# A routed feed-forward layer: gate and up computed by neuron instead of by slot

## What is computed

```python
mod = (silu(c) @ wmod).reshape(4, 6, 1, -1)          # shift, scale, gate, twice
h = layernorm(x) * (1 + ca) + sa
x = x + ga * attention(h)
h = layernorm(x) * (1 + cb) + sb
# experts: E = 8, H = 256, F = 704 neurons, top 2 of 8, weights w normalised
gate = silu(xt @ Wg[e].T)                            # (tokens, 704)
up = xt @ Wu[e].T                                    # (tokens, 704)
out = out + gate * up @ Wd[e].T * comb[:, e:e + 1]   # (tokens, 256)
x = x + gb * out
```

## Time and profile before

| | us |
|---|---|
| median of 3 runs | 262.04 (261.97 to 262.65) |
| the profiled execution, device time | 260.57 |
| its span, first to last instruction | 258.8 |
| TensorE busy | 221.5 |
| VectorE busy | 168.6 |
| ScalarE busy | 158.3 |
| GpSimd busy | 123.9 |

### The profile page before, as it was taken

One profiled execution on the slowest core, in us unless ns is written; L12 is line 12 of the kernel. 1 busy time (PEld: TensorE's weight loads), 2 busy tenths in 40 slices (PEclk: granted clock), 3 DMA queues, 4 the chain that ended last, 5 costly groups with the idle time before them and its releaser, 6 DMA issues.

```text
span 258.8 us, 5010 instructions
## 1 busy us (share of the span) xinstructions
PE 221.5 (86%) x1409; PEld 153.8 (59%) x1410; DVE 168.6 (65%) x417; ACT 158.3 (61%) x281; POOL 123.9 (48%) x172
## 2 busy tenths in 40 slices
PE   0898998989963139999999999999999999999970
PEld 0635576768852114665666666666666666666650
DVE  2347759998896996995776776769544444444430
ACT  2403999898956374888688888896444444444410
POOL 1126846778110081465666667664644454543222
PEclk9999997989965557999999999999999999999996
DMA  6998226717543046579369356233333333333111
GB/s 237 346 403 354 83 75 202 252 67 228 174 187 104 18 129 259 172 223 305 38 174 305 60 166 197 41 61 57 68 63 61 64 64 61 61 62 62 23 20 20
DMA packets 15203, 35.88 MB, mean 139 GB/s; under 512 B 1928, under 2 KB 9480, under 8 KB 15180
## 3 DMA queue, kind: packets, MB, share of 16 engines
q1 hardware_dynamic: 8424, 24.00, 27.0%
q0 software_dynamic: 5152, 9.08, 18.1%
q10 hardware_dynamic: 1604, 2.52, 2.8%
HBM read 30.47 MB, written 6.18 MB: 142 GB/s over the span
## 4 chain that ended last, share of the span: by engine, by line
PE 67%; DVE 11%; ACT 9%; DMA 5%; issue 4%; POOLq 1%; POOL 1%; ACTq 1%; DVEq 0%
PE bank L717 33%; PE bank L743 17%; PE bank L727 6%; PE bank L544 3%; ACT W L795 3%; ACT W L788 3%; PE bank L533 2%; DMA W<-in_wmod 2%; PE bank L707 2%; DMA out<-shared,dest_i 1%; PE bank L490 1%; PE bank L499 1%; DMA token_rows<-rows 1%; ACT W L801 1%; PE bank L481 1%
## 5 line engine op out<-in xcount | busy, mean ns | idle before, releaser
L717 PE MATMUL bank<-W,x 128*128 x414 | 87.9, 367 | 1.2 <-ACT x L924 1.2
L717 PEld LDWEIGHTS bank<-W,x 128*128 128x128 f16 x414 | 41.0, 99 | 41.8 <-issue 4.2
L1426 POOL DMA_INDIRECT out<-shared,dest_i x23 | 36.5, 1587 | 58.1 <-DVE shared L1289 58.1
L743 PE MATMUL bank<-W,shared 128*128 x414 | 49.7, 273 | 2.6 <-DVE shared L1304 1.7
L930 ACT ACTIVATE x<-bank,unscale 128x256 f32<-128x256 f32 (+1 forms) x69 | 31.3, 459 | 31.9 <-PE bank L717 31.9
L1279 DVE SCALAR_TENSOR_TENSOR shared<-bank,unscale,x 128x256 f32<-128x256 f32 (+1 forms) x69 | 30.7, 459 | 24.6 <-ACT x L930 24.3
L743 PEld LDWEIGHTS bank<-W,shared 128*128 128x128 f16 x414 | 39.5, 99 | 8.4 <-issue 3.0
L999 DVE SCALAR_TENSOR_TENSOR W<-staged,w_scale_bits,W 128x1408 f16<-128x1408 f32 (+1 forms) x24 | 42.4, 1766 | 1.0 <-ACT W L795 0.7
L795 ACT ACTIVATE W<-staged,w_scale_bits 128x1408 f16<-128x1408 f32 (+1 forms) x24 | 36.0, 1502 | 2.7 <-DVE w_scale_bits L980 1.6
L788 ACT ACTIVATE W<-staged 128x1408 bf16<-128x1408 f32 (+1 forms) x24 | 33.8, 1411 | 0.0
L1304 DVE TENSOR_TENSOR shared<-bank,shared 128x512 f16<-128x512 f32 (+1 forms) x46 | 23.5, 553 | 10.2 <-ACT shared L939 10.1
(11 more groups left out here) (171 smaller groups left out, 288.1 us busy)
## 6 DMA issues: line engine op xcount, KB each, us to landing
staged<-in_w SPq DMA_DIRECT2D x16, 704.0 KB, 5.2
staged<-in_w SPq DMA_DIRECT2D x8, 768.0 KB, 4.5
token_rows<-mod_rows ACTq DMA_DIRECT2D x1, 1036.0 KB
x<-in_x SPq DMA_DIRECT2D x4, 256.0 KB, 9.6
W<-in_wmod SPq DMA_DIRECT2D x2, 512.0 KB, 9.0
out<-x SPq DMA_DIRECT2D x4, 256.0 KB, 3.6
token_rows<-rows SPq DMA_DIRECT2D x4, 256.0 KB, 3.0
W<-in_w_in ACTq DMA_DIRECT2D x1, 896.0 KB, 7.4
```

The costliest lines, as they stand in the source:

```text
L717: mm = pe.matmul(bank[2 + n][:, 0:2 * w], half[:, kc * P:(kc + 1) * P], W1_pairs[:, bass.ds(e * 2 + part, 1), :, kc, n * PIECE:n * PIECE + w],
L743: mm = pe.matmul(bank[7][:, 0:D], a[:, fc * P:(fc + 1) * P], W2_16[:, bass.ds(e * 2 * W2_EXP + part * W2_EXP + fc * D, D)], start=(k == 0) ...
L1426: po.indirect_dma_start(out, bass.IndirectOffsetOnAxis(dest_i[:, j:j + 1], 0), y_sb[r], None, bounds_check=last_row, oob_is_err=True, comp ...
```

## The change

The diff does three things.

1. **Gate and up by neuron.** In `gate_up` 128 neurons of the weights are now the stationary operand and the 128 slots stream. A tile needs 11 chunks of 128 neurons (5.5 of gate, 5.5 of up; one chunk in the middle holds the last 64 of gate and 64 of up), each with 6 matmuls of 128 columns: 66 matmuls. The result has neurons on the partitions, so `turn_act` is gone. `act_hi` and `act_lo` are now made from `act` in SBUF by ScalarE and VectorE, in two sets of buffers, and `down` is 17 matmuls in another order, with waits inside it. It writes bank 5 or 7 in turn.
2. **One scale.** The largest bound over the four batches (`common_scales`) gives one scale for all rows. The three constants no longer travel with the rows; GpSimd's `unscales` and `slot_weights` read them from SBUF.
3. **Slots by VectorE.** `slot16` of the tiles 1 to 22 is copied from PSUM by VectorE after `mult_pieces`, instead of by ScalarE after SiLU.

```diff
@@ gate_up @@
-                terms = [(half, kc, part) for kc in range(DC) for half, part in ((slot_hi, 0), (slot_hi, 1), (slot_lo, 0))]
-                for n, w in enumerate(PIECES):
-                    for k, (half, kc, part) in enumerate(terms):
-                        mm = pe.matmul(bank[2 + n][:, 0:2 * w], half[:, kc * P:(kc + 1) * P],
-                                       W1_pairs[:, bass.ds(e * 2 + part, 1), :, kc, n * PIECE:n * PIECE + w],
-                                       start=(k == 0), stop=(k == len(terms) - 1))
+                for n in range(PIECES):
+                    if not (isinstance(i, int) and 4 * i + c < 1):
+                        pe.wait_ge(s["act_ok"], ACT_OPS * (4 * i + c - 1) + (ACT_OPS if n == PIECES - 1 else n + 1))
+                    for col, of in chunks[n]:
+                        terms = [(half, kc, part) for kc in range(DC) for half, part in ((slot_hi, 0), (slot_lo, 0), (slot_hi, 1))]
+                        for k, (half, kc, part) in enumerate(terms):
+                            mm = pe.matmul(bank[2 + n][:, col:col + P],
+                                           W1_16[:, bass.ds(e * 2 * W1_EXP + part * W1_EXP + kc * W1_ROW + of, P)],
+                                           half[:, kc * P:(kc + 1) * P], start=(k == 0), stop=(k == len(terms) - 1))
                     mm.then_inc(s["gu_done"], 1)
-
-            def turn_act(i, c):
...
@@ down @@
-                terms = [(a, fc, part) for a, part in ((act_hi, 0), (act_hi, 1), (act_lo, 0)) for fc in range(FC)]
+                hi, lo = act_hi[c % 2], act_lo[c % 2]
+                terms = [(hi, fc, part) for fc in range(FULL) for part in (0, 1)] + [(lo, fc, 0) for fc in range(FULL)]
+                terms += [(hi, FULL, part) for part in (0, 1)]
...
@@ ScalarE, tile_step @@
-                if not last(i, c):
-                    slots_out(i, c + 1)
...
-                sc.wait_ge(s["at_done"], 2 * (4 * i + c) + 1)
-                sc.activation(act_hi[:, 0:4 * P], bank[5][:], ACT.Copy).then_inc(s["act_hi_ok"], 1)
-                sc.wait_ge(s["at_done"], 2 * (4 * i + c) + 2)
-                sc.activation(act_hi[:, 4 * P:6 * P], bank[6][:, 0:2 * P], ACT.Copy).then_inc(s["act_hi_ok"], 1)
+                if not (isinstance(i, int) and 4 * i + c < 2):
+                    sc.wait_ge(s["down_done"], 4 * i + c - 1)
+                for cols, ready in ((slice(0, 2 * PIECE), PIECES - 1), (slice(2 * PIECE, FC * P), ACT_OPS)):
+                    sc.wait_ge(s["act_ok"], ACT_OPS * (4 * i + c) + ready)
+                    sc.activation(act_hi[c % 2][:, cols], act[:, cols], ACT.Copy).then_inc(s["act_hi_ok"], 1)
@@ VectorE @@
+            def common_scales():
+
+                ve.wait_ge(s["scale_in"], 16)
+                most, inverse = bounds[:, B:B + 1], bounds[:, B + 1:B + 2]
+                link(ve.tensor_reduce(most, bounds[:, 0:B], AX.X, ALU.max))
+                link(ve.reciprocal(inverse, most))
+                ve.tensor_scalar(common[:, G_ROW:G_ROW + 1], inverse, ROW_NORM, None, ALU.mult)
...
             def tile_step(i, c):
                 mult_pieces(i, c)
+                if not last(i, c):
+                    ve.wait_ge(s["xt_done"], 4 * i + c + 2)
+                    ve.tensor_copy(slot16, slots_p).then_inc(s["slot_ok"], 1)
...
+                lows(i, c)
                 if c == 0:
                     slot_weights()
-                else:
-                    result(i, c - 1, (c - 1) % 2)
...
+                if c:
+                    result(i, c - 1, (c - 1) % 2)
@@ GpSimd, unscales @@
-                po.wait_ge(xs_in[j % 4], 16 * (j // 4 + 1))
```

More of the change, by code:

```diff
@@ L27 @@
 GATE = D
[L28 to L33, removed]
-W1_MAT = DC * F
+ROW_ALL = 2 * D
+BOUND = 2 * D
+MODROW = BOUND + 1
+FULL = F // P
+REST = F - FULL * P
+PIECE = 2 * P
+PIECES = 3
+W1_MAT = DC * F
+W1_ROW = 2 * F
+MIXED = FULL * P
+UP_FROM = F + REST
+ACT_OPS, LOW_OPS = 4, 3
+G_UNSCALE, G_UP, G_BACK, G_ROW = range(4)
 W1_EXP = 2 * W1_MAT
@@ L128, in laid_out @@
                             by_partition(np.ascontiguousarray(router_w.T)), b_out.reshape(DC, P).T], axis=1)
[L129 to L132, removed]
+    rest_first = np.concatenate([np.arange(MIXED, F), np.arange(MIXED)])
+    turned = [np.concatenate([by_partition(np.ascontiguousarray(m.T)) for m in (Wg[e], Wu[e][rest_first])], axis=1)
+              for e in range(E)]
+    down = [by_partition(np.concatenate([Wd[e].T, Wd[e].T[MIXED:]], axis=0)) for e in range(E)]
     w_in_t = np.concatenate([W_in.T, W_in[:P][pairs].T], axis=1)
@@ L171, in layer @@
         xn2 = [sb(f"second_xn{r}", TB * D) for r in range(2)] + xn
-        row_scale = sb("row_scale", B)
+        bounds = sb("bounds", B + 2)
+        common = sb("common", 4)
         shift_out = sb("shift_out", DC * B)
@@ L331, in layer @@
             sumsq_ok norm_done wscale_ok hi_ok lo_ok
-            gu_done sig_ok act_ok xt_done slot_ok slot_weight_ok unscale_ok at_done act_hi_ok act_lo_ok down_done y_ok""".split()
+            gu_done sig_ok act_ok xt_done slot_ok slot_weight_ok unscale_ok act_hi_ok act_lo_ok down_done y_ok""".split()
         s = {n: sem(n) for n in names}
@@ L373, in at_tile, with y_bank @@
             return table.get(c, []) if isinstance(i, int) and i == 0 else []
+        def y_bank(c):
+            return bank[5 if c % 2 == 0 else 7]
         def last(i, c):
@@ L1141, in _ @@
             second_normed(0)
+            common_scales()
             power_scale(0, W2_OF)
@@ L1276, in mult_pieces, with lows @@
             def mult_pieces(i, c):
-                for n, w in enumerate(PIECES):
-                    ve.wait_ge(s["sig_ok"], len(PIECES) * (4 * i + c) + n + 1)
-                    ve.scalar_tensor_tensor(act[:, n * PIECE:n * PIECE + w], bank[2 + n][:, w:2 * w],
-                                            unscale[c % 4][:, 1:2], sig[:, n * PIECE:n * PIECE + w],
-                                            ALU.mult, ALU.mult).then_inc(s["act_ok"], 1)
+                if not (isinstance(i, int) and 4 * i + c < 1):
+                    ve.wait_ge(s["act_lo_ok"], LOW_OPS * (4 * i + c))
+                parts = [(0, slice(0, P), bank[2][:, 2 * P:4 * P], slice(0, PIECE)),
+                         (1, slice(0, P), bank[3][:, 2 * P:4 * P], slice(PIECE, 2 * PIECE)),
+                         (2, slice(0, P), bank[4][:, 2 * P:3 * P], slice(MIXED - P, MIXED)),
+                         (2, slice(0, REST), bank[4][REST:P, P:2 * P], slice(MIXED, FC * P))]
+                for n, rows, up, cols in parts:
+                    ve.wait_ge(s["sig_ok"], PIECES * (4 * i + c) + n + 1)
+                    ve.scalar_tensor_tensor(act[rows, cols], up, unscale[c % 4][rows, 1:2], sig[rows, cols],
+                                            ALU.mult, ALU.mult).then_inc(s["act_ok"], 1)
+            def lows(i, c):
+                hi, lo = act_hi[c % 2], act_lo[c % 2]
+                ve.wait_ge(s["act_hi_ok"], 2 * (4 * i + c) + 1)
+                cols = slice(0, 2 * PIECE)
+                ve.tensor_tensor(lo[:, cols], act[:, cols], hi[:, cols], ALU.subtract).then_inc(s["act_lo_ok"], 1)
+                ve.wait_ge(s["act_hi_ok"], 2 * (4 * i + c) + 2)
+                cols = slice(2 * PIECE, MIXED)
+                ve.tensor_tensor(lo[:, cols], act[:, cols], hi[:, cols], ALU.subtract).then_inc(s["act_lo_ok"], 1)
+                cols = slice(MIXED, FC * P)
+                ve.tensor_tensor(hi[REST:P, cols], act[0:REST, cols], hi[0:REST, cols], ALU.subtract).then_inc(s["act_lo_ok"], 1)
             def result(i, c, r):
```

106 lines of the change are left out of this document (49 added, 57 removed).

## The result

The changed kernel takes 326.5 us (median of 4 runs, 323.51 to 326.87) against 262.0 us before (260.86 to 262.65). The ratio is 1.243, with a 95% interval of 1.237 to 1.249. The prediction was 325, in a range of 308 to 343.

The account below looks back on a forecast made before the run. TensorE's array was taken to bound the kernel before, its sequencer the changed one at 9.5 us a tile. Expert stage +61.2, tail +1.1 and first half +0.3 on 260.57 gave 323.2; with the median 1.5 higher, 325 us, range 308 to 343.

## What to carry to other kernels

Count the instructions of the sequencer as well as the matmuls. An address worked out at run time costs TensorE 0.13 us here whatever it loads, so a rearrangement that cuts long streams into short ones multiplies a cost that no busy row shows; take additions together into fewer instructions before judging it. And a fast bound hides nothing: when a bottleneck is removed, read again who releases each gather and each buffer, since orders that were harmless under a 9.4 us tile cost some 18 us under one of 6 (280.0 to 257.6, less the 4.8 of the addresses in `down`).

## What the runs showed of the hardware

- One register instruction with four additions is busy for 55 ns, one with one address for 46, and the next starts 133 ns behind the one at the least and 124 behind the other. In these streams a register instruction costs its busy time plus 78 ns, so most of the price is the instruction, not the arithmetic.
- 66 pairs of a 128-column f16 weight load and a 128-column matmul ran in 3.86 us, 56 ns from start to start, stretch after stretch, with loads of 95 to 98 ns fully hidden.
- Waits of 1.5, 1.9 and 2.7 us on TensorE were each followed by a `gate_up` at less than the full granted clock (5.5, 5.5 and 6.3 us instead of 3.7 to 3.9), which about doubled their cost; behind another of 2.2 us there was none of it. What decides that was not settled.
